# Queries and keys of blocks 13 to 15 projected once, their rows doubled by DMA

## What is computed

```python
q = jax.nn.silu(x @ Wq); k = jax.nn.silu(x @ Wk); v = x @ Wv
q, k, v = (split(q), split(k), split(v))        # 16 heads of 8
q = _lrpe(q, theta)                             # concat [t*cos(ang), t*sin(ang)]
k = _lrpe(k, theta)
energy = jnp.einsum('bhnd,bhmd->bhnm', q, k) * mask
out = jnp.einsum('bhnm,bhmd->bhnd', energy, v)
out = out.transpose(0, 2, 1, 3).reshape(b, n, d) @ Wo
out = out * jax.nn.sigmoid(x @ G1 @ G2)
# attention output normed, x + it normed again: x1
shared = jax.nn.silu(x @ sg) * (x @ su) @ sd
return shared + SCALE * routed.reshape(b, s, h)
```

## Time and profile before

| | us |
|---|---|
| median of 3 runs | 825.48 |
| lowest and highest run | 823.49, 828.65 |
| the profiled execution, whole | 824.92 |
| its span | 822.9 |
| PE busy | 768.0 |
| DVE busy | 586.1 |
| ACT busy | 368.4 |
| POOL busy | 405.8 |

### The profile page before, as it was taken

One profiled execution on the slowest core, in us unless ns is written; L12 is line 12 of the kernel. 1 busy time (PEld: TensorE's weight loads), 2 busy tenths in 40 slices (PEclk: granted clock), 3 DMA queues, 4 the chain that ended last, 5 costly groups with the idle time before them and its releaser, 6 DMA issues.

```text
span 822.9 us, 30732 instructions
## 1 busy us (share of the span) xinstructions
PE 768.0 (93%) x12462; PEld 625.8 (76%) x12462; DVE 586.1 (71%) x1866; ACT 368.4 (45%) x802; POOL 405.8 (49%) x395
## 2 busy tenths in 40 slices
PE   5889999999999999999998898989999999999994
PEld 3667777777777777777776676768999988899884
DVE  7488898888888898898878988744444454544675
ACT  6425554646556464554633331223323333323584
POOL 5541242523335243332534554571677778876442
PEclk9999999999999999999999999999999999999998
DMA  4155233231423323232222212113443445433555
GB/s 146 47 174 179 80 91 82 64 98 48 99 76 78 89 57 96 58 88 76 69 73 63 61 33 67 46 58 128 98 86 45 89 98 105 71 50 43 128 148 145
DMA packets 71164, 70.56 MB, mean 86 GB/s; under 512 B 11444, under 2 KB 54251, under 8 KB 71025
## 3 DMA queue, kind: packets, MB, share of 16 engines
q1 hardware_dynamic: 54000, 52.33, 23.0%
q0 software_dynamic: 17024, 16.28, 11.0%
HBM read 23.99 MB, written 28.89 MB: 64 GB/s over the span
## 4 chain that ended last, share of the span: by engine, by line
PE 77%; DVE 11%; issue 4%; DMA 3%; POOL 2%; SPq 1%; ACT 1%; POOLq 0%; ACTq 0%; DVEq 0%
PE energy_banks L1932 6%; PE bank L1850 5%; PE energy_and_gate_banks L1850 5%; PE bank L1852 5%; PE bank L1851 5%; PE bank L2406 4%; PE energy_and_gate_banks L2406 4%; PE energy_and_gate_banks L1957 4%; PE energy_and_gate_banks L1852 3%; PE energy_and_gate_banks L1851 3%; PE bank L1891 3%; DVE EM L1242 3%; PE energy_banks L1850 3%; PE energy_banks L1852 3%; PE energy_banks L1851 3%
## 5 line engine op out<-in xcount | busy, mean ns | idle before, releaser
L627 POOL DMA_INDIRECT dispatched_rows<-x,slot x128 | 130.5, 1019 | 236.4 <-PE energy_banks L1932 142.8
L761 POOL DMA_INDIRECT summed_rows<-VP,goal_i x80 | 123.8, 1548 | 43.3 <-issue 22.7
L1119 ACT ACTIVATE sq<-energy_banks 128x512 f32<-128x512 f32 (+1 forms) x96 | 50.6, 527 | 120.2 <-PE energy_banks L1852 116.6
L832 ACT ACTIVATE sf<-energy_and_gate_banks 128x512 f32<-128x512 f32 x88 | 52.4, 596 | 70.5 <-PE energy_and_gate_banks L1852 69.8
L842 ACT ACTIVATE hidden_rounded<-sf 128x512 fp32r<-128x512 f32 x88 | 55.3, 628 | 52.4 <-DVE sf L1272 52.4
L1272 DVE TENSOR_TENSOR sf<-sf,bank 128x512 f32<-128x512 f32 x88 | 60.3, 685 | 18.3 <-PE bank L1852 16.8
L1932 PE MATMUL energy_banks<-EM,VP 64*32 64x64 f32 x4096 | 59.0, 227 | 2.2 <-issue 2.2
L1850 PE MATMUL energy_and_gate_banks<-xgT_hi,ws_hi 128*128 128x512 f32 x108 | 51.7, 479 | 9.9 <-DVE EM L1242 9.3
L1242 DVE TENSOR_TENSOR EM<-energy_and_gate_banks,causal 128x512 f32<-128x512 f32 x64 | 44.1, 688 | 20.1 <-PE energy_banks L1957 20.0
L1932 PEld LDWEIGHTS energy_banks<-EM,VP 64*32 64x32 f32 x4096 | 47.6, 106 | 5.4 <-issue 4.6
L1850 PE MATMUL bank<-xgT_hi,ws_hi 128*128 128x512 f32 x108 | 45.5, 421 | 3.6 <-DVE QM L1789 1.7
(11 more groups left out here) (256 smaller groups left out, 2189.4 us busy)
## 6 DMA issues: line engine op xcount, KB each, us to landing
QM<-QT SPq DMA_DIRECT2D x248, 32.0 KB
dispatched_rows<-empty POOLq DMA_DIRECT2D x8, 655.0 KB, 4.2
QM<-dispatched_rows SPq DMA_DIRECT2D x8, 655.0 KB, 5.6
QT<-sq SPq DMA_DIRECT2D x40, 128.0 KB, 2.8
KT<-sq SPq DMA_DIRECT2D x40, 128.0 KB
xin<-in_x SPq DMA_DIRECT2D x16, 256.0 KB, 2.9
QM<-summed_rows SPq DMA_DIRECT2D x16, 256.0 KB, 2.8
out_x<-QM SPq DMA_DIRECT2D x16, 256.0 KB, 3.2
```

Of the source, the lines that this page charges most:

```text
L627: g.indirect_dma_start(out=xg_d, out_offset=bass.IndirectOffsetOnAxis(ap=slot[:, n % 2, j:j + 1], axis=0), in_=x1[:, n % 2, j % NC, :], in ...
L761: g.indirect_dma_start(out=sum_d, out_offset=bass.IndirectOffsetOnAxis(ap=goal_i[:, par, t:t + 1], axis=0), in_=ye[:, par, t, :], in_offse ...
```

## The change

Blocks 13 to 15 join those that are projected once. PE's and ACT's calls for i = 2 and 3 are taken out of steps 12 to 14, DVE's `turn` for those blocks becomes the one in place, SP's `double` runs in those steps, and three waits are fitted to the new counts. Nothing is moved otherwise.

```diff
--- before.py
+++ after.py
@@ -331,7 +331,7 @@
 
         def projected_once(f):
 
-            return within(f, 3, DIRECT + 2)
+            return within(f, 3, B - 1)
 
         def no_ffn(b):
 
@@ -798,8 +798,6 @@
                     return
                 need(act, pe_qk, 4 * f + i + 1)
                 need(act, v_qk, 4 * f + i - 1)
-                if f == DIRECT + 3:
-                    need(act, once_ld[i % 2], 64 * DIRECT)
                 if f == 0 and i == 0:
                     act.wait_ge(v_wq, 1)
                 a.activation(sq[:, i % 2], PB[i % 2][:], ACT.Silu).then_inc(a_silu, 1)
@@ -999,8 +997,6 @@
                         silu(f, fp, 1)
                         copy_out(b, 1, par)
                         shared_silu(b, s0, SPARE)
-                        silu(f, fp, 2)
-                        silu(f, fp, 3)
                         values(f, fp, 0)
                         hidden_hi(b, s0, SPARE)
                         values(f, fp, 1)
@@ -2172,8 +2166,6 @@
                         logits(b)
                         states_and_out(2)
                         shared_pair(s0, SPARE)
-                        project(f, 2)
-                        project(f, 3)
                         energies_and_state(2)
                         values_projected(0)
                         values_projected(1)
@@ -2239,7 +2229,7 @@
                 need(pe, v_x1, 4 * (b - 1))
                 need(pe, a_kt, 2 * last(b) + 2)
                 if DIRECT + 2 < b < B - 1:
-                    need(pe, a_silu, 4 * b + 6)
+                    need(pe, a_silu, 4 * b + 8)
                 need(pe, v_lg, b - 2)
                 if b == B:
                     need(pe, v_pos, b)
@@ -2262,7 +2252,7 @@
             def logits(b):
 
                 need(pe, a_x1T, b - 1)
-                need(pe, a_silu, 4 * last(b + 1) + (0 if shared_turn(b) is not None else 2))
+                need(pe, a_silu, 4 * last(b + 1) + (0 if shared_turn(b) is not None else 4 if b < B - 1 and projected_once(b + 1) else 2))
                 for c in range(NC):
                     ins = t.matmul(PB[1][:, 8 * c:8 * c + 8], x1T[:, P * c:P * (c + 1)], rwt_s[:], start=True, stop=True)
                 ins.then_inc(pe_lg, 1)
```

## The result

The changed kernel takes **846.85 us** (median of 4 runs, 846.2 to 848.18) against 827.07 us for the kernel before beside it on the same chip (823.49 to 830.29): a ratio of 1.0247, 95% interval 1.0215 to 1.0279, so 2.5% slower. The forecast was 846.0 us, with a range of 839 to 853. Measured once more, on another chip, the changed kernel takes 847.93 us (6 runs) against 824.57: a ratio of 1.0271 (1.0244 to 1.0298). The two intervals overlap.

The account below looks back on a forecast made before the run. It took PE and DVE both near their limit, PE waiting for DVE's masks. Terms 1.6 (step 12) + 10.8 (step 13) + 6.6 (step 14) + 1.5 (clock) = 20.5 us on the 825.48 us median: 846.0 us, range 839 to 853.

Parts of the forecast that it names:

- PE's share: PE busy 93% of the span; forecast counted 0.80 us won from removed matmuls in step 12, 0 in steps 13 and 14.
- The rival that counted them: Steps 12 to 14: doubling hidden, the 18 removed matmuls win 4.35 us, total 821.1 us; chance 5%.
- The queue on SP decides: Steps 12 to 14: doubling waits behind SP's earlier instructions, costing +10.8 us in step 13, +6.6 in step 14; chance 85%.
- Predicted delays of mask 1: DVE's mask of energies 1, needed by PE, comes 2.4, 10.8 and 6.6 us late in steps 12, 13 and 14.
- Only the latency, not the queue: SP starts doubling at the silu's end; masks late by 1.6, 1.9 and 1.7 us, total 830.7 us; chance 5%.
- The give-back of 0.80 us in step 12: Removed matmuls ahead of energies 2 take back DVE's 0.80 us wait, so the 2.4 us delay costs +1.6.
- The clock: +1.5 in step 13: TensorE's clock falls after an idle stretch of about 10 us, adding 1.5 us from mask to logits' copy.
- paid already: Step 14's mask-to-logits stretch already ran at low clock in the earlier profile, so its added clock loss was 0.
- The sum: Steps 12 to 14: delays and clock add 20.5 us to the kernel before, giving 846.0 us, 2.5% slower.
- PE stays slow: Each stall leaves 1.2 GHz from mask to logits in all three steps, about 8 us more: 854 us; chance 5%.

Follow-up runs that it names:

- the first experiment: The changed kernel with SP issuing both doublings before the input load, stores and reload in steps 12 to 14: 835.35 us, ratio 1.0104 to the kernel before.
- both moves: The changed kernel with SP's doublings ahead of load and stores, and DVE's first turn behind mask 1 and the gated product: 825.35 us, ratio 0.9993.
- the control: The kernel before with only DVE's first turn moved behind mask 1 and the gated product, four projections, no doubling: 824.5 us, ratio 0.9991.

## Why the prediction was right, point by point

**PE's share is not what binds: right.** The 18 matmuls are worth nothing that the medians show (0.9988 without any doubling, 0.9993 with all of it hidden), and 0.7 us in step 12 by the marks. The rival that counted them (821.1 us) is ruled out by that interval, not only by the result.

**The queue on SP decides: right, with one addition.** Predicted delays of mask 1 against the start of the silu were 2.4, 10.8 and 6.6 us. Measured from the timelines (silu start to mask 1): 6.73 against 4.68 us in step 12, 15.10 against 4.58 in step 13, 11.06 against 4.87 in step 14, so 2.05, 10.5 and 6.2. The three differ from the forecast by 0.3 to 0.4 each, all to the same side, and that is the latency: I took 5.3 us from first issue to the usable row, and it was 4.7 to 4.9, at the low end of the 4.75 to 5.75 from the earlier trace rows. In steps 13 and 14 SP came free 0.2 to 0.3 us later behind the silu than forecast, which hid part of that. The addition is that SP's order is only half of the mechanism: the loss needs a late DMA and a consumer that stands ahead of the mask on DVE. Either one mended alone leaves 10 us; both, none.

**Only the latency, not the queue (830.7 us): mis-sized.** That condition was made in the first experiment and gave 835.35. The delays were nearly as I had priced them (5.4 against 5.2 us in all); what I had left out of the rival is the clock, which falls behind PE gaps of about 2 us as well.

**The give-back of 0.80 us in step 12: not had.** I expected +1.6 there (2.4 less 0.80). From mask 1 to mask 2 the step took 431.71 - 424.48 = 7.23 us, against 6.90 in the earlier trace rows, although six matmuls were gone: the clock was at 0.50 from 426, behind a PE gap of 2.4 us. The step cost 2.35 us more by its marks. The give-back is real at full clock: with both moves, step 12 is 0.7 us shorter than in the control.

**The clock: +1.5 in step 13 measured at +1.4, and a second loss missed.** From mask to logits step 13 took 466.30 - 459.85 = 6.45 us against 5.07. In step 14, which I had counted as paid already, it took 7.20 against 6.54, so 0.7 more. Step 14's loss in the earlier trace rows was not a fixed cost: it is absent in the kernels whose windows show the clock at 1.00, where that stretch took 5.1.

**The sum.** From the forecast's 20.5 take 1.1 for the three delays and 0.1 for step 13's clock, and add 1.1 for step 12 (a give-back of 0.80 that was a loss of 0.33) and 0.7 for step 14's clock: 21.1. The marks show 19.3, since step 15 was 1.7 us shorter than before (16.30 against 17.98); nearly all of that is a pause of 1.48 us on PE that the profiled execution of before happened to have, so it is no gain. Between the medians it is 19.8, and 23.4 in the second measurement, so how close 846.0 lies to 846.85 is partly luck: the sizes were wrong by 1.2 us one way and 1.8 the other, and two measurements of the same pair differ by 3.6 us.

**PE stays slow (854 us): no.** The slow stretch did not last from mask to logits in step 13; the clock was back at 1.00 by 464, 2 us ahead of the logits' copy.

## What to carry to other kernels

SP's program and DVE's are run in the order in which they are written, so before a transfer is added, read what stands ahead of it in that queue and what stands behind its consumer in the consumer's queue: a pattern that is hidden in ten blocks cost 12 us in block 14, where a load that waits, a store and its landing stood ahead and a mask that TensorE needs stood behind. Work taken off the busiest engine was worth nothing in the two steps where the other engine has no wait behind it; the timelines of those steps say so, the page's share doesn't. And price a stall on TensorE with its clock: here a gap of 2 us cost as much again in the matmuls behind it.

## What the runs showed of the hardware that I had not expected

- The granted clock fell to 0.50 (1.2 GHz) around PE gaps of only about 2 us: in the first experiment in steps 12, 13 and 14 (gaps of 2.45, 1.96 and 1.92 us, the last two shortly behind pauses of 1.23 and 1.08 us), for 3 to 6 us each time. Mask to logits in step 13 was 7.50 us there, longer than behind the 10.5 us gap of the changed kernel (6.45): the short stall cost more clock time than the long one, where part of the slow time passes while PE has nothing to do.
- It also falls by chance where nothing differs: in step 14 of the kernel before, and in that of the kernel without doubling (window 0.93 from 466 to 491), not in that with block 13 alone (1.00); and so from 60 to 80 us, where all kernels have the same code: four profiles show 0.67 or 0.68 there, that of the kernel before 0.95. This, and pauses of about 1.4 us on PE in which it waits for nothing that the profile shows, make differences of 1 to 3 us between executions of the same code. What starts such a pause is open.
- The doubling's latency is even within the changed kernel: 4.68 to 4.90 us from the first of four issues to the turn, in all three steps. With SP's order changed it is 4.91 to 5.50 us, and with only DVE's turns moved 5.77 in step 13, where the four issues take 3.51 us instead of 2.65. Why they take longer there isn't shown.
